# Self-attention scores from queries and keys split in high and low parts, with the maxima added by a third product, in a kernel of four transformer layers

## What is computed

```python
x = x + xattn(layernorm(x), ctx_1024, itok)   # 4 transformer layers
x = x + window_attention(layernorm(x))        # 16 earlier tokens, sigmoid weights
x = x + ternary_ffn(layernorm(x))             # 1024 wide, rounded to 8 bits and to -1, 0, 1
```

```python
h = rmsnorm(x, n1[l]); q, k, v = split(h @ Wqkv[l].T + bqkv[l])
q, k = rope(q), rope(k)
s = einsum('bhqd,bhkd->bhqk', q, k) * 0.25 + causal_bias
x = x + merge(softmax(s) @ v) @ Wo[l].T + bo[l]
h2 = rmsnorm(x, n2[l])          # then cross-attention, within a window of 128 context tokens
x = x + cross(h2, ctx_1024) @ Wo_c[l].T
h3 = rmsnorm(x, n3[l])
x = x + (silu(h3 @ Wg[l].T) * (h3 @ Wu[l].T)) @ Wd[l].T
```

## Time and profile before

| what | number |
|---|---|
| median of three runs | 584.85 us |
| the profiled execution: span from first to last instruction | 584.8 us |
| PE busy | 528.3 us, 90% |
| weight loads (beside PE) | 409.0 us |
| DVE busy | 356.2 us, 61% |
| ACT busy | 282.2 us, 48% |
| POOL busy | 116.2 us, 20% |
| mean granted clock of PE | 0.982 of full speed |

### The profile page before, as it was taken

The page is one execution under the profiler, slowest core; times in us unless marked ns, Lnnn a source line. Parts: engine busy times, 40 slices in busy tenths (PEclk is TensorE's granted clock), DMA queues, the critical chain, the costliest instruction groups (busy, mean ns, idle before and its releaser), DMA issues.

```text
span 584.8 us, 15276 instructions
## 1 busy us (share of the span) xinstructions
PE 528.3 (90%) x6585; PEld 409.0 (70%) x6586; DVE 356.2 (61%) x669; ACT 282.2 (48%) x509; POOL 116.2 (20%) x125
## 2 busy tenths in 40 slices
PE   4988898999998988999998989999989989899765
PEld 2666665988676656988766649987766669887514
DVE  5977356566564655665745474573755546752796
ACT  1165654623346456433445636243574666326542
POOL 5241200022332100021622000021621001621100
PEclk9999999999999999999999989999999989999977
DMA  8300080010500100200501200203101100000001
GB/s 324 151 2 2 3 322 4 14 61 1 217 38 3 39 36 3 73 0 2 216 2 39 75 1 1 73 1 142 76 7 31 67 2 1 1 0 2 2 2 40
DMA packets 4682, 30.38 MB, mean 52 GB/s; under 512 B 1153, under 2 KB 1665, under 8 KB 2818
## 3 DMA queue, kind: packets, MB, share of 16 engines
q1 hardware_dynamic: 4610, 29.35, 13.5%
HBM read 28.82 MB, written 0.52 MB: 50 GB/s over the span
## 4 chain that ended last, share of the span: by engine, by line
PE 73%; DVE 13%; ACT 9%; issue 2%; POOL 1%; DVEq 0%; ACTq 0%; POOLq 0%
PE psD L345 15%; PE QD L688 13%; PE psD L701 10%; PE QD L442 7%; DVE AQ L1904 5%; PE QD L482 5%; ACT PTR L1331 4%; PE psD L339 3%; PE psD L502 3%; PE psD L688 2%; PE psD L523 2%; PE psD L509 2%; PE QD L475 2%; PE psD L383 2%; DVE MX L1901 2%
## 5 line engine op out<-in xcount | busy, mean ns | idle before, releaser
L1331 ACT ACTIVATE PTR<-QD 128x2048 f32<-128x2048 f32 x40 | 74.9, 1873 | 56.4 <-PE QD L482 47.5
L1904 DVE TENSOR_REDUCE AQ<-QD 128x8 f32<-128x2048 f32 (+1 forms) x24 | 55.0, 2291 | 27.7 <-PE QD L442 27.5
L688 PE MATMUL QD<-HH,WFH 128*128 128x256 f32 x224 | 69.1, 309 | 1.7 <-DVE WFL L2008 1.7
L2605 POOL TENSOR_TENSOR rstd<-ms,mhalf 128x2 f32<-128x2 f32 x26 | 19.2, 737 | 250.0 <-DVE ms L1827 246.8
L688 PE MATMUL QD<-HL,WFH 128*128 128x256 f32 x224 | 63.3, 283 | 0.0
L688 PE MATMUL QD<-HH,WFL 128*128 128x256 f32 x224 | 63.3, 283 | 0.0
L1901 DVE TENSOR_REDUCE MX<-QD 128x16 f32<-128x2048 f32 x16 | 36.7, 2293 | 39.6 <-PE QD L442 39.6
L2008 DVE TENSOR_TENSOR WFL<-WC,WFH 128x512 fp32r<-128x512 f32 x64 | 46.5, 757 | 20.0 <-ACT WFH L1377 19.4
L701 PE MATMUL psD<-WC,HID 128*128 128x256 f32 x256 | 58.5, 382 | 0.0
L345 PE MATMUL psD<-WAB,hT 128*128 128x256 f32 (+1 forms) x152 | 53.2, 488 | 0.9 <-DVE hT L1842 0.9
L701 PEld LDWEIGHTS psD<-WC,HID 128*128 128x128 f32 x256 | 47.6, 190 | 7.2 <-issue 1.0
(11 more groups left out here) (186 smaller groups left out, 992.2 us busy)
## 6 DMA issues: line engine op xcount, KB each, us to landing
WC<-in_wc SPq DMA_DIRECT2D x4, 3072.0 KB, 10.2
WAB<-in_wa SPq DMA_DIRECT2D x4, 1024.0 KB, 6.4
WAB<-in_wb SPq DMA_DIRECT2D x4, 1024.0 KB, 4.8
WF<-in_wf SPq DMA_DIRECT2D x1, 3072.0 KB, 11.3
bias<-in_bias SPq DMA_DIRECT2D x4, 512.0 KB, 5.7
WAB<-in_wt SPq DMA_DIRECT2D x1, 1024.0 KB, 7.4
X<-in_x SPq DMA_DIRECT2D x2, 256.0 KB, 2.7
out_x<-X SPq DMA_DIRECT2D x4, 128.0 KB, 2.4
```

The costliest lines, as they stand in the source:

```text
L688: mm = pe.matmul(S[:, w * L:(w + 1) * L], wp[:, m, :], hp[:, k, :], start=(k == 0 and j == 0), stop=(k == KT - 1 and j == 2))
L1331: nc.scalar.activation(PTR[:, r % 2, :], QD[:, :], ACT.Exp, scale=SCALE if r < SELF_ROUNDS else 1.0).then_inc(t_exp, 1)
L1904: v = dve.tensor_reduce(QKR[b][:, t, 0, h, MAXROW].rearrange("p (s r) -> p r s", r=SG_H), QD[:, :].rearrange("p (r s n) -> p r s n", r=4, ...
```

## The change

Queries and keys are split into a part rounded to F32R and the rest. POOL splits the queries, into the two halves of a head's 32 columns; DVE writes each key twice, so that a transposed head has 16 rows of queries high and 16 of queries low against the key twice. ACT's copy out of PSUM rounds both to F32R (tile SPLIT), and DVE subtracts the rounded key from the one in PSUM (`key_low_strips`), which is now what frees the bank. A score is two F32R products in the same 32 rows: with the high part of the keys, and with the low part.

The maxima have no column among the queries any more. DVE writes them high and low into a tile MS; one transpose takes them all, and `scores_T` adds them with a third product, against a constant SEL of zeros and ones. It waits for the copy of the maxima only ahead of this third product.

Some small tensors share memory with others now, pads of AQ are no longer cleared at the start, and the four lists have a new order in many places. The core of the diff (lines of `if cross` branches that only move are left out):

```diff
             def rotated_T(l, b, t, m):
                 pe.wait_ge(qr_set[b], l * QT + t + 1)
+                pe.wait_ge(qsplit_set[b], l * QT + t + 1)
...
             def scores(l, r):
-                            mm = pe.matmul(quad[a][:, at:at + keys], QKT[b][rows(a), s, q * P:(q + 1) * P],
-                                           QKT[b][rows(a), s, L:L + keys], start=False, stop=True, skip_group_check=True)
+                        for k_high in (True, False):
+                            for a in range(4):
+                                mm = pe.matmul(quad[a][:, at:at + keys], SPLIT[b][rows(a), s, 0, t * P:(t + 1) * P],
+                                               SPLIT[b][rows(a), s, 1, 0:keys] if k_high else key_low(b, s)[rows(a), 0:keys],
+                                               start=False, stop=True, skip_group_check=True)
...
             def maxima_T(l, r):
+                    pe.wait_ge(m_low, l * SELF_ROUNDS + r + 1)
-                    for n, s in enumerate(ss):
-                        mm = pe.transpose(bank(l, use)[:, n * P:(n + 1) * P], block_of(b, t, 0, s), ident)
+                    mm = pe.transpose(bank(l, use)[:, 0:P], MS[:, r % 2, :], ident)
...
             def scores_T(l, r):
-                pe.wait_ge(*emptied(l, f"q2_{r}"))
-                            for a in range(4):
-                                mm = pe.matmul(quad[a][:, at:at + P], QKT[b][rows(a), s, L + k * P:L + (k + 1) * P],
-                                               Q2[rows(a), n * P:(n + 1) * P], start=(at == 0), stop=True, skip_group_check=True)
+                            for k_high in (True, False):
+                                for a in range(4):
+                                    pe.matmul(quad[a][:, at:at + P],
+                                              SPLIT[b][rows(a), s, 1, keys] if k_high else key_low(b, s)[rows(a), keys],
+                                              SPLIT[b][rows(a), s, 0, t * P:(t + 1) * P],
+                                              start=(at == 0 and k_high), stop=False, skip_group_check=True)
+                    pe.wait_ge(sel_set, 1)
+                    pe.wait_ge(*emptied(l, f"q2_{r}"))
+                    for n in range(len(ss)):
+                        at, keys = n * (t + 1) * P, (t + 1) * P
+                        for a in range(4):
+                            mm = pe.matmul(quad[a][:, at:at + keys]..., SEL[rows(a), n:n + 1].broadcast_to([STRIP, P]),
+                                           MT[rows(a), r % 2, :]..., start=False, stop=True, skip_group_check=True)
...
             def self_strips(l, b, t, m):                       # ACT
-                nc.scalar.activation(QKT[b]..., bank(l, use)..., ACT.Copy).then_inc(free(l, use), 1)
+                nc.scalar.activation(SPLIT[b][:, 2 * m:2 * m + 2, :, t * P:(t + 1) * P], bank(l, use)..., ACT.Copy).then_inc(khi_set[b, t, m], 1)
...
             def add_sines(l, b, t):                            # DVE
-                dve.memset(QKR[b][:, t, 0, :, MAXROW], 0.0)
-                dve.tensor_tensor(rotated(b, t), rotated(b, t), RT[b][:, t, :]..., ALU.add).then_inc(qr_set[b], 1)
+                dve.tensor_tensor(r[:, 0, :, :], QKR[b][:, t, 0, :, 0:HD], r[:, 0, :, :], ALU.add).then_inc(qsum_set[b], 1)
+                dve.tensor_tensor(QKR[b][:, t, 1, :, :]..., QKR[b][:, t, 1, :, HD:STRIP]..., r[:, 1, :, :]..., ALU.add).then_inc(qr_set[b], 1)
+            def key_low_strips(l, b, t, m):                    # DVE
+                dve.wait_ge(khi_set[b, t, m], l + 1)
+                dve.tensor_tensor(KLOW[b][m][:, :, keys], bank(l, use)..., SPLIT[b][:, 2 * m:2 * m + 2, 1, keys],
+                                  ALU.subtract).then_inc(free(l, use), 1)
...
             def maxima(l, r):                                  # DVE, self-attention
+                    dve.tensor_reduce(m, QD..., AX_X, ALU.max, negate=True).then_inc(s_max, 1)
+                    dve.tensor_copy(to[:, :, 0:n].bitcast(F32R), m).then_inc(m_high, 1)
+                    dve.wait_ge(m_high, l * SELF_ROUNDS + r + 1)
+                    dve.tensor_tensor(to[:, :, 4:4 + n], m, to[:, :, 0:n], ALU.subtract).then_inc(m_low, 1)
...
+            def split_queries(l, b, t):                        # POOL
+                pool.wait_ge(qsum_set[b], l * QT + t + 1)
+                nc.gpsimd.tensor_copy(high.bitcast(F32R), of).then_inc(qhi_set[b], 1)
+                pool.wait_ge(qhi_set[b], l * QT + t + 1)
+                nc.gpsimd.tensor_tensor(low, of, high, ALU.subtract).then_inc(qsplit_set[b], 1)
...
                 scale_ternary(0)
-                rsqrt(NL - 1, 2, 1)
+                scale_ternary(1)
                 weigh_last(0)
-                scale_ternary(1)
```

## The result

The changed kernel is slower: 606.56 us (median of four runs, 602.53 to 609.98), 1.035 times the kernel before (95% interval 1.030 to 1.040). The forecast was 592.4, its range up to 600. The direction was right; the size was a third of what came (+7.6 against +21.6).

The account below looks back on a forecast made before the run. The kernel was taken as bound by PE (busy 90% of the span), with DVE the bound at the start of layer 0. 584.8 + 3.2 (layer 0) + 2.7 (layers 1 to 3) + 1.7 (tail) = 592.4 us, range 579.5 to 600.

Parts of the forecast that it names:

- Rival B: PE's 128-column F32R waves take 0.064 instead of 0.11, saving 13.6 us over four layers; 578.8 us, chance 0.07.
- the bound of 2.4: Lower end of layer 0's +2.4 to +3.9: DVE's added 3.9 ahead of `scores_T`, part hidden by 1.46 of slack.
- What follows in layer 0 I leave at zero: Layer 0 behind its start: two maxima copies leaving the chain (about 0.3 each) against third products of 0.24 each; no change.
- the four waits: Layer 2 replay, PE waiting at `rotated_T` 0.75, `scores_T(3)` 1.8, `pv(3)` 0.95, `cross_q` 1.2: 4.7 against 2.39 idle, +2.3.
- The sign that was named: Layer 2: the stage from `scores(0)` to `scores(6)` 1 to 2 us longer, PE waiting for POOL's split and causal cut.
- The 0.6 per layer that I took back from the cross-attention: Layers 1 to 3: 0.6 of 2.59 idle in the cross stage recovered, since DVE and ACT reach it relatively earlier.
- two thirds of one wait and half of the other: Tail: 2.5 of PE's 3.7 idle behind the last norm's scaling, and 1.2 of DVE's 2.5 ahead of the window attention.
- The gain of 1.0 from ACT's ternary work: Tail: ACT's ternary work, moved forward into the FFN, was to give about 1.0 us.
- Nothing gets between two such operations: Tail: with two POOL scalings back to back no DVE operation gets between; reason for taking +1.7, nearer the full amounts.
- A: The waits are covered: PE's -3.2 stands, the tail's 1.75 stall goes, layer 0 pays 2.4; 582.3 us, chance 0.19.
- C: The 16 splits on POOL hold up DVE, about 0.85 per operation met, 9 us over the forecast; 601.4 us, chance 0.16.
- D: Little changes: PE's -3.2 stands, layer 0 costs +1.6, the tail +1.7; 584.9 us, chance 0.08.

Follow-up runs that it names:

- before_fill: Kernel before, with constant transposes filling PE's waits ahead of the FFN's norms and in five places of the ternary FFN; 583.0 us, ratio 0.9971.
- fill_all: Changed kernel, lists as they are, with constant transposes filling PE's waits of 1.2 us and more up to the end; 597.5 us, ratio 1.023.
- no_key_low: Changed kernel without DVE's 32 subtractions for the low parts of the keys, the second product taking the high part again; 603.7 us, ratio 1.029.
- fill: Changed kernel with 12 and 11 constant transposes in two PE waits of layer 0; 601.3 us, ratio 1.027.
- tail_bo_fill: Changed kernel with POOL's old tail order, its bias addition behind the query splits, and PE waits filled up to the last FFN; 593.4 us, ratio 1.015.
- bo_later: Changed kernel with POOL's output-bias addition moved behind the query splits in layers 0, 2 and 3; 606.0 us, ratio 1.036.

## Why the prediction was wrong

The miss is 14.2 us, and it adds up: layer 0 +3.0 (6.2 for 3.2), layers 1 to 3 +3.8 (6.5 for 2.7), the tail +1.6 (3.3 for 1.7), the difference of span and time 1.8, and 4.0 from the fastest execution, which was profiled, to the median. The parts by stage hold falls of the clock in either kernel. The two filled kernels keep most of them out (length of each stretch in the profiles):

| stretch | before_fill | fill_all | difference | forecast |
|---|---|---|---|---|
| to the transposes | 14.95 | 14.09 | -0.86 | none |
| from there to layer 0, round 6 | 53.05 | 56.25 | +3.20 | +3.2 |
| to layer 1, round 6 | 125.21 | 125.60 | +0.39 | +0.9 |
| to layer 2, round 6 | 124.49 | 127.75 | +3.26 | +0.9 |
| to layer 3, round 6 | 123.93 | 127.30 | +3.37 | +0.9 |
| to the first window scores | 82.51 | 85.46 | +2.95 | tail +1.7 |
| to the end | 56.27 | 57.26 | +0.99 | (in the tail) |

- **PE's products: right.** No gain at 128 columns, -0.4 at 256, +0.38 and +0.22 for the third product (0.45 and 0.24 forecast). Rival B is refuted by 1.07 against 1.10.
- **The clock: the step that failed first.** "The granted clock is 1.00 in the stages of the change, and I leave it there" read the clock of a stage whose waits the same text lengthened. Filled, the change costs 597.5 - 583.0 = 14.5 us by medians of two sets, or 13.3 by spans (593.7 and 580.4). It is 21.6 as it runs. The remaining 7 to 8 us are the clock, which stands at half for longer in the changed kernel: 0.958 to 0.980 in the mean over its four executions, 0.981 to 0.991 over those of before beside before_fill.
- **Layer 0: both terms wrong (6.0 from the transposes for 3.2).** `scores_T(0)` was to come 3.2 us later and came 2.0 later, below the bound of 2.4. The low parts of the keys, 1.7 of that sum, are worth 0.4 there (no_key_low). "What follows in layer 0 I leave at zero" then failed by 3.95 (41.14 for 37.19); with the waits filled it comes back to 37.87 (fill) and 37.20 (tail_bo_fill), so nearly all of it is the clock behind the waits. The +3.20 of the table meets the forecast by luck, since fill_all still has falls at 26 and 54 us; without a fall tail_bo_fill has +1.8.
- **Layers 1 to 3: the four waits right, one place missing; this is the largest error in the waits (7.0 for 2.7).** In layer 2 the four waits were forecast as 0.75, 1.8, 0.95 and 1.2 and measured 0.75, 1.54, 0.77 and 1.04, and from round 2 to round 6 PE idles 4.67 us where it idled 2.44 (+2.2 for +2.3). But the replay began at `scores(0)`. Ahead of it PE waits 1.58 us in layer 2 and 2.19 in layer 3, where it did not wait before: 0.88 and 1.14 at the rotated queries of tile 0, 0.70 and 1.05 at those of tile 1, which the new list has moved there. bo_later shows that 1.1 of each layer is POOL's bias addition standing in front of the split. The sign that was named, a stage from `scores(0)` to `scores(6)` 1 to 2 us longer, did not come (+0.4 in layer 2, none in layers 1 and 3), since the loss lies ahead of it. The 0.6 per layer that I took back from the cross-attention did not come either: from round 6 to round 9 a layer gains 0.03 to 0.14.
- **Tail: the mechanism right, the sizes wrong (3.3 to 3.9 for 1.7).** The scaling that was to stand "some 4 us" stands 4.05. I then took two thirds of one wait and half of the other; the second came whole (2.78 for at most 2.5), the first at 1.90: 1.90 + 2.78 - 1.75 = 2.9, the loss ahead of the window scores. The gain of 1.0 from ACT's ternary work, a term without a row, did not come: behind the first window scores it is +0.45, or +0.99 with both kernels filled. "Nothing gets between two such operations" is not how the two scalings went: the two DVE operations take 2.07 and 2.06, one beside each scaling (1.98 and 2.01).
- **Rivals.** A fails: the waits were not covered. C named 601.4 and the right engine pair, but DVE is held up by POOL's bias additions, causal cuts and scalings, hardly by the splits (three times 0.2 us); it is DVE that holds up the splits' casts. Leaving the splits out did not help. D fails.

Open: what the splits on POOL cost, since taking them away moves other work; why layer 0 comes 2.0 us later at `scores_T(0)` with so little of it from the low parts; and at which waits the clock falls in the slower executions, which left no profile.

## What to carry to other kernels

Where PE is the bound, a wait can have a second price, the clock behind it: count the waits of a microsecond and more that a change makes, not the sum of idle time alone. Before a stage's start is compared between executions, take off what the start of the program differs by. A replay of an order has to begin at the last point where old and new lists agree. And with DVE and POOL tightly interleaved, price each pair that can overlap by the rows where they did, since taking an operation from one moves the next onto the other.

## What the runs showed of the hardware

- Work that computes nothing can pay: transposes of a constant in PE's waits made the kernel before 0.3% faster (clock 0.982 to 1.000 in the profiles) and the changed one 1.6% (0.980 to 0.994).
- In the eighteen profiles half speed began within 1.5 us of the end of a PE wait, on either side of it, in 6 of 273 waits of 0.6 to 1.0 us, 25 of 213 of 1.0 to 1.7, and 48 of 101 longer ones. The same wait of 1.5 us ahead of the FFN's norm had half speed behind it in two layers of before (347 and 473 us) and not in the other two.
- A DVE operation that met a POOL operation ended 0.1 to 0.6 us behind it in the rows shown. Where POOL operations ran back to back, DVE came between two scalings in the changed kernel (2.07 and 2.06 us), but one DVE scaling stood through both clearings of pads (2.32 us).
